# A gated linear attention and channel-mix block on one core: four score products of a block's levels folded into two

## The reference

```python
q = silu(h @ wq); k = sigmoid(h @ wk); v = h @ wv; f = 1 - k      # 4 heads of 128
theta = cumsum(sign(f - 0.5)) * pi                                # cos = +-1, sin about 0
# for each token t, head by head:
S = S * f[t][:, None] + k[t][:, None] * v[t][None, :]             # state 128 x 128
o = (q[t] * scale) @ S
out = o * sigmoid(h @ wg1 @ wg2); out = layernorm(out) * norm_w; out = out @ wo
```

## Time and profile before

| | us |
|---|---|
| median of 3 runs (1871.46 to 1873.3) | 1872.35 |
| the profiled execution's own time | 1875.95 |
| its span, first to last instruction | 1874.0 |
| PE busy | 1838.9 (98%) |
| DVE busy | 1393.5 (74%) |
| ACT busy | 737.2 (39%) |
| POOL busy | 377.9 (20%) |
| one attention block in the middle (609.36 to 648.52) | 39.16 |

### The profile page before, as it was taken

How to read it: one execution, slowest core, us unless ns; L and a number is a source line. 1 busy time by engine, 2 the same in 40 slices (tenths; PEclk the granted TensorE clock), 3 DMA queues, 4 the chain that set the end, 5 groups by cost and what they waited for, 6 DMA issues and landing times. The chain is left out here.

```text
span 1874.0 us, 56458 instructions
## 1 busy us (share of the span) xinstructions
PE 1838.9 (98%) x24873; PEld 1649.0 (88%) x24873; DVE 1393.5 (74%) x2821; ACT 737.2 (39%) x1425; POOL 377.9 (20%) x309
## 2 busy tenths in 40 slices
PE   6899999999999999999999999999999999999998
PEld 5788989999899998999989999897898898888887
DVE  5677776777777777677776777779778778778775
ACT  3333343333333334333343333443444544544543
POOL 1011001110010100111001110012244344344343
PEclk9999999999999999999999999999999999999999
DMA  7002000010000100001000010001111111111110
GB/s 281 3 9 84 25 25 25 24 47 25 25 25 24 45 27 25 24 25 48 25 25 24 25 48 25 24 28 65 68 57 57 68 57 57 68 57 56 68 57 34
DMA packets 42650, 84.88 MB, mean 45 GB/s; under 512 B 2324, under 2 KB 2856, under 8 KB 42408
## 3 DMA queue, kind: packets, MB, share of 16 engines
q1 hardware_dynamic: 41336, 79.18, 12.0%
q10 hardware_dynamic: 1072, 2.10, 0.3%
HBM read 47.72 MB, written 33.55 MB: 43 GB/s over the span
## 5 line engine op out<-in xcount | busy, mean ns | idle before, releaser
L130 POOL TENSOR_TENSOR ln_rs<-ln_ve,mhalf 128x2 f32<-128x2 f32 x64 | 71.3, 1114 | 1016.8 <-DVE ln_ve L125 1016.8
L331 POOL TENSOR_TENSOR xs<-xs,y 128x512 f32<-128x512 f32 x64 | 83.5, 1305 | 369.5 <-DVE y L711 369.5
L1103 PE MATMUL bank<-hT_hi,wq_hi 128*128 128x256 f32 x512 | 152.2, 297 | 4.5 <-DVE wq_lo L1047 4.5
L744 DVE TENSOR_TENSOR Tot<-Tot 128x256 f32<-128x256 f32 (+2 forms) x192 | 46.9, 244 | 143.2 <-PE lvl L1180 113.3
L1103 PE MATMUL bank<-hT_hi,wk_hi 128*128 128x256 f32 x512 | 151.6, 296 | 0.0
L136 DVE TENSOR_SCALAR xn<-xs,ln_mv,ln_rs 128x512 f32<-128x512 f32 x128 | 124.5, 1013 | 29.5 <-POOL ln_rs L130 29.5
L1103 PE MATMUL bank<-hT_lo,wq_hi 128*128 128x256 f32 x512 | 146.1, 285 | 0.0
L1103 PE MATMUL bank<-hT_hi,wq_lo 128*128 128x256 f32 x512 | 145.9, 285 | 0.0
L1103 PE MATMUL bank<-hT_hi,wk_lo 128*128 128x256 f32 x512 | 145.7, 285 | 0.0
L1103 PE MATMUL bank<-hT_lo,wk_hi 128*128 128x256 f32 x512 | 145.5, 284 | 0.0
L1103 PE MATMUL bank<-xk_hi,fk_hi 128*128 128x256 f32 x512 | 145.1, 283 | 0.2 <-DVE xk_lo L843 0.2
(11 more groups left out here) (180 smaller groups left out, 5708.0 us busy)
## 6 DMA issues: line engine op xcount, KB each, us to landing
xs<-in_L_attn_x SPq DMA_DIRECT2D x32, 512.0 KB, 3.6
x_scratch<-xs SPq DMA_DIRECT2D x32, 512.0 KB, 3.2
xs<-x_scratch SPq DMA_DIRECT2D x32, 512.0 KB, 3.5
out<-xs SPq DMA_DIRECT2D x31, 512.0 KB, 2.8
mod_raw<-in_L_wmod SPq DMA_DIRECT2D x6, 1024.0 KB, 13.2
raw_q<-in_L_attn_wq SPq DMA_DIRECT2D x1, 1024.0 KB, 10.3
raw_k<-in_L_attn_wk SPq DMA_DIRECT2D x1, 1024.0 KB, 13.5
raw_v<-in_L_attn_wv SPq DMA_DIRECT2D x1, 1024.0 KB, 10.0
```

What stands on the lines that cost most here:

```text
L130: pool.tensor_tensor(out=ln["rs"][:, :], in0=ln["ve"][:, :], in1=mhalf[:, :], op=ALU.pow).then_inc(ln["rstd"], 1)
L331: pool.tensor_tensor(out=dst, in0=dst, in1=y[:, ch, :], op=ALU.add).then_inc(x2_sb, 1)
L744: dve.tensor_tensor(out=Tot[:, off2:off2 + cnt2], in0=t[:, :, 0], in1=t[:, :, 1], op=ALU.mult)
L1103: last = pe.matmul(dst, lhs(a, s), rhs(b, s), start=(t == 0), stop=(t == len(terms) - 1))
```

## The change

- **Two levels in one product.** `PAIRS = (2, 8)`. For m = 2 and m = 8, `pair_product` does levels m and 2m at once: 32 matmuls whose moving operand has 48 columns, three quarters of each 4m tokens, once from Q and once from a new area `X` between the two Q buffers. `variants` writes X (three multiplications of 256 numbers a partition), before the product. `pair_update` then brings Q and K over both levels (three quarters each, six multiplications of 256), and `pair_merge` puts the scores in place with five predicated copies.
- **Decay tables.** `first_totals`, `neighbours` and `joint` form the tables; the first two for the next block, ahead of `apply_next`, in the block before.
- **Order on VectorE.** `first_update` and `variants` run before `diagonal`; `gated_stats(n, 1)` moves behind them into the next block; `f_signed`, `q_odd` come later. The crossing is reordered likewise.
- **Order on TensorE.** There is no product between the second q and the first k rows, nor between the second k and the first v rows.
- **Loads.** SyncE waits for one weight load to land before it issues the one after next. `mod_product` 4 and 5 move to block 5, their loads to blocks 2 and 3; W_k and W_r are loaded in block 6 by SyncE, not in block 2 by ScalarE. Some buffers get other addresses.

```diff
+                def pair_product(n, par, i):
+                    m = PAIRS[i]
+                    pe.wait_ge(x_set, 2 * n + i + 1)
+                    pe.wait_ge(level, NU * n + i + 1)
...
+                            rhs = QX[:, g, b, 32 * par:32 * par + 64].rearrange("p (s four m) -> p s four m", four=4, m=m)[:, :, 1:4, :]
+                            last = pe.matmul(dst[quad, :, g, :], K[par][:, g, quad], rhs, start=True, stop=True)
+                    last.then_inc(mm["lvl"], 1)
...
+                def variants(n, par, i):
...
+                    dve.tensor_tensor(out=x[:, :, :, 1, :], in0=q[:, :, :, 3, :], in1=spread_over(t[:, :, 2], m), op=ALU.mult)
+                    dve.tensor_tensor(out=x[:, :, :, 2, :], in0=q[:, :, :, 2, :], in1=spread_over(t[:, :, 1], m), op=ALU.mult)
+                    dve.wait_ge(tabs, 9 * n + 4 * i + 2)
+                    dve.tensor_tensor(out=x[:, :, :, 3, :], in0=q[:, :, :, 3, :], in1=spread_over(d[:, :, 1], m), op=ALU.mult
+                                      ).then_inc(x_set, 1)
...
-                    level_product(n, par, 2)
+                    pair_product(n, par, 0)
                     wait(pe, s_mid, n)
                     rows_of("q", 1, 2, "q")
                     if n == 0:
-                        mod_product(3, bank[1])
-                    level_product(n, par, 3)
+                        mod_product(2, bank[1])
...
                     rows_of("k", 0, 4, "k")
-                    if n == 0:
+                    if n == 5:
+                        pe.wait_ge(ogt_lo, 2 * n)
                         mod_product(4, bank[1])
-                    level_product(n, par, 4)
+                    pair_product(n, par, 1)
                     pe.wait_ge(h_full, 4 * (n + 2))
                     rows_of("k", 1, 4, "k")
...
-                    level_product(n, par, 5)
...
+                    first_update(n, par)
+                    variants(n, par, 0)
                     diagonal(n, par)
+                    first_merge(n, par)
+                    if n > 0:
+                        gated_stats(n - 1, 1)
+                    joint(n, 0)
...
+                    level_update(n, par, 64, 5)
+                    q_odd(n + 1, 1 - par)
+                    ln_var(dve, ln, n + 2)
+                    first_totals(n + 1)
                     apply_next(n + 2)
                     g1_low(n + 1)
...
                 mod_load(SA)
+                sp.wait_ge(mod_in[CA], 16)
                 rows_in(w_raw["q"], env["wq"], w_in["q"])
+                sp.wait_ge(mod_in[SA], 16)
                 rows_in(w_raw["k"], env["wk"], w_in["k"])
-                sp.wait_ge(mod_cols, 1)
+                sp.wait_ge(w_in["q"], 16)
                 rows_in(w_raw["v"], env["wv"], w_in["v"])
```

More of the change, by code:

```diff
@@ L254, in blocks @@
             sem(ctx, n) for n in ("halo", "diff", "xk_f", "xr_f", "xk_lo_s", "xr_lo_s", "sq", "ka_lo_s", "rv"))
-        r_gb, x3 = (sem(ctx, n) for n in ("r_gb", "x3"))
+        r_gb, x3, x_set, tabs = (sem(ctx, n) for n in ("r_gb", "x3", "x_set", "tabs"))
         def level_bank(idx, par):
@@ new lines, in attention_body @@
+                        ogt_low(n - 1, 0)
+                        ogt_low(n - 1, 1)
+                    else:
+                        centre_wo()
+                    neighbours(n, 1)
+                    pair_update(n, par, 0)
+                    variants(n, par, 1)
+                    pair_merge(n, par, 0)
+                    q_silu(n + 1, 1 - par, 0)
+                    joint(n, 1)
+                    q_silu(n + 1, 1 - par, 1)
+                    pair_update(n, par, 1)
+                    pair_merge(n, par, 1)
@@ L1089, in _ @@
                 dve.wait_ge(mod_set, 3)
+                for i, m in enumerate(PAIRS):
+                    first_half = masks[:, 1 + 2 * i, :].rearrange("p (n two m) -> p n two m", two=2, m=m)[:, :, 0, :]
+                    for j in range(2):
+                        dve.tensor_copy(twice[:, i, :].rearrange("p (n two m) -> p n two m", two=2, m=m)[:, :, j, :], first_half)
                 h_high(1)
@@ L1161, in near_scores @@
                             quad = slice(32 * b, 32 * b + 32)
-                            last = pe.matmul(near(par)[quad, g, :], K[par][:, g, quad], Qx[par][:, g, b, :], start=True, stop=True)
+                            last = pe.matmul(near(par)[quad, g, :], K[par][:, g, quad], QX[:, g, b, 48 * par:48 * par + 48],
+                                             start=True, stop=True)
+                    last.then_inc(mm["lvl"], 1)
+                def pair_product(n, par, i):
+                    m = PAIRS[i]
+                    pe.wait_ge(x_set, 2 * n + i + 1)
+                    pe.wait_ge(level, NU * n + i + 1)
+                    if i == 0:
+                        wait(pe, merged_act, 3 * n)
+                    else:
+                        pe.wait_ge(merged, NM * n + 2)
+                    dst = level_bank(2 + i, par)[:, 0:2 * G * 24].rearrange("p (s g t) -> p s g t", s=2, g=G)
+                    for g in range(G):
+                        for b in range(QB):
+                            quad = slice(32 * b, 32 * b + 32)
+                            rhs = QX[:, g, b, 32 * par:32 * par + 64].rearrange("p (s four m) -> p s four m", four=4, m=m)[:, :, 1:4, :]
+                            last = pe.matmul(dst[quad, :, g, :], K[par][:, g, quad], rhs, start=True, stop=True)
                     last.then_inc(mm["lvl"], 1)
@@ L1166, in level_product @@
                     q, k = Q[par], K[par]
-                    m = LEVELS[idx - 1]
                     pe.wait_ge(level, NU * n + idx - 1)
-                    if idx == 2:
-                        wait(pe, merged_act, 3 * n)
-                    else:
-                        pe.wait_ge(merged, NM * n + idx - 1)
+                    pe.wait_ge(merged, NM * n + (6 if idx == 4 else 10))
                     dst = level_bank(idx, par)
                     for g in range(G):
-                        if m <= 16:
-                            for b in range(QB):
-                                quad = slice(32 * b, 32 * b + 32)
-                                rhs = q[:, g, b, :].rearrange("p (n two m) -> p n two m", two=2, m=m)[:, :, 1, :]
-                                last = pe.matmul(dst[quad, g * 16:g * 16 + 16].rearrange("p (n m) -> p n m", m=m), k[:, g, quad], rhs,
-                                                 start=True, stop=True)
-                        elif m == 32:
+                        if idx == 4:
                             for b in (0, 2):
```

301 lines of the change are left out of this document (180 added, 121 removed).

## The result

| | before | after |
|---|---|---|
| median of 4 runs each | 1872.57 us (1871.46 to 1873.3) | 1830.32 us (1828.25 to 1833.06) |
| ratio, 95% interval | | 0.9776 (0.9759 to 0.9793) |
| profiled execution's own time | 1875.95 | 1829.41 |
| its span | 1874.0 | 1827.5 |
| middle attention block | 39.16 | 37.75 |

What follows compares the result with a forecast made beforehand. PE, busy 1838.9 of 1874.0 us, was taken to bound the kernel. 1874.0 - 44.6 + 1.5 - 3.6 + 2.4 = 1829.7 of span, 1831.7 with its surroundings, median 1828; range 1820 to 1843.

Steps and rivals of the forecast that it cites:

- Price of a pair product: On PE: one 48-column pair product costs 1.02 us, priced by near_scores; bounds 0.87 and 2.2.
- Per block: Attention blocks: four products of 0.87 go, two of 1.02 come, 1.44 us less; over 31 blocks -44.6 us.
- DVE fits as a total, the places decide: Middle block: DVE gets 3.5 us more, some 32.5 of 37.7; places where PE would wait decide; +1.5 us in all.
- the four places: Spare before PE waits: first pair product 0.7, second 0.6, level 32's update 1.0, gate at most 0.1 us.
- DVE late in every block: Rival: 36 new small DVE instructions each cost 0.04 us more, 0.5 beyond both covers, 31 times; 1843 us; chance 0.22.
- the 0.20 of the estimate: DVE's added work per block: ten merges taken at about 2.0 us, with two dependent steps in each five.
- Stops by issue, start and block 0: PE stops among small matmuls: block 0 gains 3.6, the start 0.7, block 0 gives back 0.7; together -3.6 us.
- the 7.9 at stake: Block 0: upper bound of the gain from its two stops and the low clock; one stop in two was let go.
- both stops fell in runs of over 170: Block 0: stops of 2.1 and 2.2 us came in runs of over 170 small matmuls; four such runs, two stops.
- Crossing: Between the layers: no gain, PE waits 2.9 us at xk_lo; +2.4 us, bounds -1.5 and +6.
- DVE is the limit here: Crossing: DVE bounds it and gets the two pairs' work too; no DVE idle time behind xk_lo until about 1310.
- Sum: Whole kernel: span 1829.7 us, 1831.7 with 1.95 around it; median 3.6 under the profiled execution, so 1828.

Runs made afterwards that it cites:

- second profile of before's code: Kernel before with only SyncE's load waits of the change added: 1871.84 us against 1872.84 of before in its group, ratio 0.9996.
- The runs above: Changed kernel with k's shift and low earlier in the crossing: 1830.8 us, ratio 0.9777; with four more DVE instructions behind low there: 1834.59 us, ratio 0.9787.

## Why the prediction was right, point by point

- **Price of a pair product** (1.02 taken, bounds 0.87 and 2.2): 1.03. Choosing `near_scores` as the nearest row, equal in count and width, was right to 0.01. The 0.15 over a 16-column product is paid nearly all with each matmul, as the choice by width has it; the edges count once for a run, so that a second product right behind the first costs 0.68.
- **Per block** (-1.44, and +0.05 at the gate): -1.42, which holds both. The chain at the gate costs 0.02, by the kernel with the tables behind it. Over 31 blocks that is -44.0 against a forecast of -43.1. The middle blocks of the second profile of before's code (39.11, not 39.17) would make it -1.36 a block, -42.2 in all: the forecast lies between.
- **DVE fits as a total, the places decide.** 32.19 us busy (32.5 forecast), distances of 0.65, 0.35, 1.08 and 0.05 at the four places (forecast as spares 0.7, 0.6, 1.0 and at most 0.1). With the 0.05 that a handover takes, the first two spares are 0.6 and 0.3 and the last is nought: PE and DVE's chain meet at the gate, and PE loses 0.02 there. The rival "DVE late in every block" was given 0.22 and didn't come. Its mechanism is real: 0.6 us at the gate cost 0.45 a block and 16 us in all. It did not come since the small instructions were no dearer than taken: merges of 64 numbers start 0.13 apart (595.23, 595.36, 595.49 are three such rows), not the 0.20 of the estimate, which made room for the tables. It was close: at the gate there was no room at all. The rival's own sum has a slip: 1.4 less the covers of 1.0 and 0.1 is 0.3 a block and not 0.5, which gives about 1838 and not 1843, the upper end of the range.
- **Stops by issue, start and block 0** (-3.6, with block 0's later `g1_lo` in it). The start came out at -1.29, of which the stop is 0.8 (0.7 forecast), in a profile at the lower end of the scatter. Blocks 0 and 5 together give -5.88, less 2 x 1.42 for the products, -3.04, where 3.6 less 0.7 was forecast. The number is right by luck, since the course of it isn't: I let one of two stops in block 0 stay. Both went, with the low clock of that stretch, and a new one of 2.2 came in block 5, in the only run of 192 small matmuls that the change makes. The long run in block 5 was named in the prediction and should have had a stop of its own. Half of the 7.9 at stake would also be 4.0 and not 3.6. And "both stops fell in runs of over 170" passes over a third: the 2.8 us of L1180 in two waits are the 2.2 in block 0 and 0.64 in block 3, in a run of 64.
- **Crossing** (+2.4): +1.71, but not in the way forecast. Up to the first row that waits for `xr_lo` PE is 3.5 later than before (26.82 behind the near product, 23.31 before), and the same 3.5 stand at the first product of `V` and `Kt` (36.54, 33.01): the prediction had a term for DVE's lateness at `xk_lo`, 2.0, and none for what comes on top up to `xr_lo`, 1.5. Some 1.0 of this is GpSimd's: one of its additions now runs (1245.53 to 1246.98) beside the four multiplications of `xr`, which take 2.69 where those of `xk` take 1.67. Then 1.8 came back that no term had, 1.5 of it in the second layer's first block, which ran at a granted clock of 1.00 and before at 0.94. That is luck: in the kernel with the tables behind the gate it didn't come back. `xk_lo` was forecast to be done 17.2 behind the near product (1290.1 less 1272.94) and is (1241.92 less 1224.73); PE's wait for it is 3.63, forecast 2.9. The sentence "DVE is the limit here" was the better one of the two that the prediction had; the wait for `xk_lo` is only where its lateness shows. The runs above showed this.
- **Sum.** 1829.7 of span forecast, 1827.5 measured: start 0.6, products and gate 0.9 and crossing 0.7 better than forecast. The first and the last of these are within what varies between profiles; the products are the part that the prediction can claim. The median is 2.3 above the forecast of it, because the profiled execution of before was 3.6 over its median and that of after was 0.9 under its own. The offset between profile and median was the largest single error, and it is of the size of the spread of runs.

## What to carry to other kernels

On an engine that is busy all the time, price a new product by the row that is equal to it in count and width, from start to next start, and check it at its edges; then walk each follower to the four or five places where the bound engine would wait, and state the spare at each. Count the handover (0.05 us here) off each spare. At the gate nothing was left of it and nearly nothing was lost, but the next 0.6 us at that place cost 16 us in all, and the same 0.6 just behind it none. Where a second engine bounds a short stretch, moving a chain forward only moves the wait; by these runs less work of that engine is what would shorten it, which no run here tried.

## What the runs showed of the hardware that was not expected

- 32 fp32 matmuls (64 in the trace) take 0.67 us from start to next at 16 moving columns, 0.68 at 24 and 0.82 at 48, with row products behind them. Inside the run they start 8.8, 8.9 and 10.8 ns apart (8.5 at 2 columns), and the end adds 0.11 to 0.14.
- By the traces TensorE waits for its own instructions in a stop by issue: all 34 stops of the 13 traces end 2.2 to 2.8 us behind the start of a 16 KB packet of the queue q8. Runs of small matmuls use up a packet's 252 instructions in 1.1 to 1.4 us. Stops of 1.5 us and more came in runs of 192 and more and once right behind one of 128, short ones (0.3 to 0.7) also in runs of 64 and 128 or right behind them. When a packet is asked for is not shown.
- A stop of 2.2 us took the granted clock from 1.00 to 0.53 for the next 3.4 us, and in the crossing with more work it was 0.95 for the 3.9 us ahead of the level product and the wait of 4.0, and 0.50 for the 4.7 behind them. That can double the price of a stop.
- The stop at the start shrank from 3.6 us to 2.8 to 3.1 in the twelve profiles with the new order of the loads.
- DVE's `xr_lo` takes 2.24 us and the equal `xk_lo` 1.23. Beside the first, GpSimd adds 512 numbers (1249.02 to 1250.32), beside the second nothing. Before, DVE's L758 of 512 numbers took 1.78 instead of 0.68 beside the same addition.
